# Writing out the steps of a biased attention with three routed trees, spacing the trees' groups four slots apart, and moving the routing of the last tree ahead of the end of the attention

## The chip, the cores and the metric

The kernel runs on one core of one Trainium2 chip. The time is the device time of one execution in microseconds (us). The kernel before was timed three times: 751.34, 752.47 and 753.41 us, median 752.47.

## What is computed

The input x is (4, 512, 128). It is normalised over its last axis (xn), and two branches are added to x.

```
xn  = (x - mean) / sqrt(var + 1e-5)
# branch 1: attention, 16 heads of 8, 512 tokens, 4 batches
q,k,v = split(xn @ w_qkv.T);  s = q.k * 8**-0.5 + bias[bucket(k_pos - q_pos)]
a     = softmax(s) @ v @ w_proj.T + b_proj
# branch 2: four hard-routed trees q, k, v, f of depth 8 (256 leaves, 16 hidden units each)
fff(x, act): node = 0; 8 times: node = 2*node + 1 + (x.nw[node] + nb[node] > 0)
             leaf = node - 255;  return act(x @ w1[leaf] + b1[leaf]) @ w2[leaf] + b2[leaf]
xm  = (xn - mean) / sqrt(std + 1e-5)
y   = xm + softmax(fff_q(xm) . fff_k(xm) / sqrt(128)) @ fff_v(xm)      # relu inside
b   = y + fff_f(y)                                                     # exact gelu inside
out = x + a + b
```

The last tree (f) works on y, so it can be routed only after the softmax over the outputs of the other three.

## The kernel before, in words

All five engines run one program each, ordered by semaphores and written out by hand. There is no planner: what stands next to what is set by small tables.

**The attention** (branch 1) is 16 steps: 4 batches times 4 groups of 4 heads (`n = 4 * b + g`). A step has 20 slots. In slots 0 to 15 TensorE computes one tile of scores of step n (`scores_k`, L1037 and L1039) for which ScalarE takes the exponent (`exps`, L824); in slots 4 to 19 it computes one tile of scores of step n + 1 (`scores_q`, L1026), of which VectorE takes the row maximum (`row_max`, L636); at slots 6, 10, 14 and 18 it multiplies by the values (`weigh`, L1049). Between two steps stand `max_rows` (L1066), `sub_max` on VectorE (L642, which every next step waits for), `split_k`, `split_q` and `normalise`; after every fourth step comes `output` (L1085, L1091). Score banks are used in pairs, so TensorE can be two tiles ahead of VectorE and of ScalarE and no more. The first 12 steps are in loops of three turns (`Fori`) on TensorE, VectorE and ScalarE, the last four steps stand written out.

**The trees** sort the 2048 tokens into 48 tiles of 128 by blocks of 8 leaves: VectorE routes (`route`, L546 to L607), TensorE counts (`ranks`, L968), GpSimd scatters the rows to DRAM with 16 indirect DMAs (`scatter`, L412). Four tiles are a group, so a tree has 12 groups. A group has four stages on TensorE: x (transposes, L1100), h (first product, L1106), m (mask, L1111), y (second product, L1116). ScalarE copies after x and takes the activation after h, VectorE masks after m and copies after y. SyncE loads the rows and the four weight blocks of a group two groups ahead (`turn`: `rows` L263, four register loads of block numbers L268, four weight DMAs L272) and stores the result (L283). GpSimd gathers a finished tree from DRAM with 16 indirect DMAs (`gather`, L417). Trees q, k and v ride in the attention's first 12 steps, three groups to a step, at the slots of `STAGES`.

**The attention of branch 2** (16 tiles, `attention`, L1158 s, L1164 p, L1177 o) rides in steps 12 to 14, a tile every two slots, after eight blocks of transposes (`qk_in`, L1129). Its `o` uses bank WB, its `p` bank 7.

**The last tree** is routed in step 15 (`y_transposed` L1137, `y_logits` L1147, `route_y` L679) and scattered after it. Its 12 groups have a schedule of their own (`F_PE`, `F_DVE`): six sets of buffers (`FG = 6`), two banks for each stage, the weight DMAs shared between SyncE and ScalarE. At the end GpSimd gathers, adding into `acc`, while SyncE stores each batch of `out` as soon as its four gathers have landed.

Of the kernel before, what the change touches and what calls it, by code (L numbers as in the profile page):

```python
# [20 lines left out]
F32 = mybir.dt.float32  # L21
F32R = mybir.dt.float32r
BF16 = mybir.dt.bfloat16
# [5 lines left out]
P = 128  # L29
# [18 lines left out]
GPS = GROUPS // NG  # L48
# [10 lines left out]
STAGES = [(0, "x0"), (2, "h0"), (4, "m0"), (5, "x1"), (6, "y0"), (8, "h1"), (10, "m1"), (11, "x2"), (12, "y1"),  # L59
          (14, "h2"), (16, "m2"), (19, "y2")]  # L60
# [9 lines left out]
          "yl": 1, "hr": 1, "hh": 1, "hm": 1, "mk": 1, "yy": 1, "st": 16,  # L70
          "f_xs": 2, "f_h": 2, "f_hr": 2, "f_hm": 2, "f_y": 2, "f_yl": 2, "f_st0": 16, "f_st1": 16}
FG = 6
F_PE = "x0 x1 h0 m0 x2 h1 m1 x3 y0 h2 m2 x4 y1 h3 m3 x5 y2 h4 m4 y3 h5 m5 y4 y5".split()
F_DVE = "x0 x1 x2 m0 x3 m1 y0 x4 m2 y1 x5 m3 y2 m4 y3 m5 y4 y5".split()
# [8 lines left out]
def attend(delays, tree, g, at):  # L83

    if tree is not None:
        return []
    return [(k, sum(ATT_TILES[:g]) + r) for r in reversed(range(ATT_TILES[g])) for k, d in delays.items()
            if ATT_FROM[g] + 2 * r + d == at]
# [5 lines left out]


def stages(tree, g, at):

    return [] if tree is None else [(what[0], GPS * g + int(what[1])) for slot_, what in STAGES if slot_ == at]

# [7 lines left out]
def build(nc, x, wq, wk, wv, wp, bp, table, onehot, cf, cb, nw, nb, wl, b2, out):  # L107
# [7 lines left out]
    with ctx:  # L115
        def sb(name, shape, dt=F32):
# [58 lines left out]
        end = strip[:].rearrange("p a b -> p (a b)").bitcast(F32)  # L175
        nw_f, nb_f = end[:, 0:NODES], end[:, NODES:2 * NODES]
        bits_f, work_f = end[:, 1024:3072], end[:, 3072:5120]
# [10 lines left out]

        f_wt = end[:, 0:FG * GT * WROW].rearrange("p (q t c) -> p q t c", q=FG, c=WROW)
        f_xl = yt[:].rearrange("p a b c -> p (a b c)")[:, 0:FG * GT * ROW].rearrange("p (q t c) -> p q t c", q=FG, c=ROW)  # L190
        f_xTs, f_hr, f_hm, f_yl = (tuple(pt[:, k // 2, k % 2 * 2 + i].rearrange("p (t c) -> p t c", c=P)
                                         for i in range(2)) for k in range(4))

        ps = ctx.enter_context(nc.psum_tensor("ps", [P, 8, NS], F32))
        OB, WB = 4, 6
# [1152 lines left out]
```

## Time and profile before

| | us |
|---|---|
| median of three runs | 752.47 |
| the profiled execution, its own time | 751.0 |
| its span, first to last instruction | 748.9 |
| TensorE busy | 576.3 (77%) |
| VectorE busy | 455.4 (61%) |
| ScalarE busy | 299.5 (40%) |
| GpSimd busy | 254.9 (34%) |
| mean granted TensorE clock | 0.90 |

Busy time of TensorE is modelled and counts overlapping work as full, so a row of instructions is best read by the distance of their starts. "PEld" is a weight load of TensorE, "DVE" VectorE, "ACT" ScalarE, "POOL" GpSimd, "SPq" the queue of SyncE. "L412" is line 412 of the kernel.

### The profile page before, as it was taken

To read this page: it belongs to the slowest core of one execution; us is meant where nothing else is said; L and a number is where in the kernel's file an instruction comes from. 1 tells how busy PE (TensorE), PEld (TensorE's weight loads), DVE (VectorE), ACT (ScalarE), POOL (GpSimd) and SP (SyncE) were. 2 spreads that over 40 slices of the span, in tenths; PEclk is the share of its full clock that TensorE was granted. 3 is DMA by queue.
4 is the path that set the end of the run, shared out by engine and by line. 5 is a ranking of instruction groups with operands and counts; after the bars stand their busy time and mean duration, and the time that the engine had idled before them with its cause. 6 is when DMAs were issued, how large, how long until landed. Compare 5 with 4: busy or idle time off the path is not lost.

```text
span 748.9 us, 12769 instructions
## 1 busy us (share of the span) xinstructions
PE 576.3 (77%) x3522; PEld 417.0 (56%) x3540; DVE 455.4 (61%) x1036; ACT 299.5 (40%) x703; POOL 254.9 (34%) x239
## 2 busy tenths in 40 slices
PE   1185465999999999999999999994999996174800
PEld 0173332666776667667667676663666674074800
DVE  3979887576676667776667767752656667033500
ACT  4510010655555446546455465471555523021300
POOL 4403667710000768700183000084000000787075
PEclk9786876999999999999999999997999999576955
DMA  7979341444344466744475443121000000779333
GB/s 219 271 164 277 125 118 46 110 128 124 104 113 114 122 170 141 147 113 112 105 146 128 117 110 94 51 36 22 1 0 1 1 15 4 221 173 303 88 46 68
DMA packets 108825, 83.30 MB, mean 111 GB/s; under 512 B 8688, under 2 KB 105840, under 8 KB 108768
## 3 DMA queue, kind: packets, MB, share of 16 engines
q1 hardware_dynamic: 89952, 66.91, 33.0%
q0 software_dynamic: 15104, 12.63, 9.1%
q10 hardware_dynamic: 3712, 3.16, 1.5%
q14 instruction: 41, 0.34, 0.2%
q8 instruction: 16, 0.26, 0.1%
HBM read 58.30 MB, written 24.36 MB: 110 GB/s over the span
## 4 chain that ended last, share of the span: by engine, by line
PE 44%; issue 21%; POOL 7%; DVE 4%; ACT 3%; DMA 2%; SPq 2%; DVEq 0%; POOLq 0%; ACTq 0%
PE ps L1049 7%; PE ps L1026 6%; PE ps L1037 6%; PE ps L1039 6%; PE ps L1106 5%; PE ps L1116 3%; PE ps L1009 3%; POOL acc L417 3%; DVE ps L636 2%; POOL yt L417 2%; PE ps L1100 2%; POOL xs L412 2%; DMA ys<-pt 1%; PE ps L1262 1%; ACT hr L835 1%
## 5 line engine op out<-in xcount | busy, mean ns | idle before, releaser
L636 DVE CUSTOM_DVE_ANT_0 ps<-ps,strip 128x512 f32<-128x512 f32 x256 | 176.9, 704 | 116.7 <-PE ps L1026 112.5
L824 ACT ACTIVATE pt<-ps 128x512 f32<-128x512 f32 x256 | 148.9, 603 | 96.1 <-PE ps L1039 94.1
L412 POOL DMA_INDIRECT xs<-xr,slot x64 | 63.3, 990 | 254.7 <-issue 137.6
L417 POOL DMA_INDIRECT yt<-ys,slot x48 | 74.2, 1547 | 155.3 <-DMA ys<-yl 141.3
L1037 PE MATMUL ps<-qs,km 128*128 128x512 f32 x256 | 121.5, 475 | 3.3 <-ACT pt L824 1.7
L1026 PE MATMUL ps<-km,qs 128*128 128x512 f32 x256 | 108.2, 436 | 11.9 <-DVE qs L619 5.4
L1039 PE MATMUL ps<-u_lo,rev_r 128*128 128x220 f32 (+1 forms) x256 | 74.3, 290 | 0.0
L1039 PE MATMUL ps<-u_hi,rev_r 128*128 128x220 f32 (+1 forms) x256 | 72.8, 284 | 0.0
L1049 PE MATMUL ps<-pt,v_aug 128*32 128x512 f32 x512 | 68.2, 605 | 0.7 <-ACT pt L824 0.7
L1026 PEld LDWEIGHTS ps<-km,qs 128*128 128x128 f32 x256 | 48.7, 194 | 35.0 <-DVE mx L636 27.5
L1037 PEld LDWEIGHTS ps<-qs,km 128*128 128x128 f32 x256 | 48.8, 191 | 17.4 <-ACT pt L824 9.7
L1039 PEld LDWEIGHTS ps<-u_lo,rev_r 128*128 128x128 f32 x256 | 48.2, 188 | 11.3
L835 ACT ACTIVATE hr<-ps,wt 128x128 f32<-128x128 f32 x144 | 41.2, 369 | 31.9 <-PE ps L1106 31.9
L417 POOL DMA_INDIRECT yt<-in_b,leaf x48 | 46.0, 958 | 19.6 <-issue 14.0
L1039 PEld LDWEIGHTS ps<-u_hi,rev_r 128*128 128x128 f32 x256 | 49.0, 191 | 4.1 <-issue 2.2
L1116 PEld LDWEIGHTS ps<-wt,hm 128*128 128x128 f32 x288 | 36.8, 191 | 11.1 <-issue 10.1
L1106 PEld LDWEIGHTS ps<-xTs,wt 128*128 128x128 f32 x288 | 35.9, 191 | 12.6 <-issue 12.0
L1106 PE MATMUL ps<-xTs,wt 128*128 128x128 f32 x288 | 39.4, 280 | 1.7 <-ACT xTs L830 1.7
L1116 PE MATMUL ps<-wt,hm 128*128 128x128 f32 x288 | 39.2, 279 | 0.0
L965 PE MATMUL ps<-v_all,yt 128*128 128x256 f32 x96 | 26.9, 440 | 13.8 <-DVE pt L594 8.7
L636 DVE DVE_READ_ACCUMULATOR2_ANT mx<- 128x1 f32 x256 | 36.3, 142 | 0.0
L671 DVE COPY yl<-ps 128x512 f32<-128x512 f32 x36 | 24.9, 692 | 16.9 <-PE ps L1116 15.2
(218 smaller groups left out, 903.5 us busy)
## 6 DMA issues: line engine op xcount, KB each, us to landing
wt<-in_wl SPq DMA_DIRECT2D x144, 128.5 KB
xl<-xs SPq DMA_DIRECT2D x36, 258.0 KB
ys<-yl SPq DMA_DIRECT2D x36, 256.0 KB, 2.8
xs<-mx SPq DMA_DIRECT2D x2, 3096.0 KB, 22.8
strip<-bias_bf SPq DMA_DIRECT2D x1, 3584.0 KB, 36.4
yt<-xs SPq DMA_DIRECT2D x12, 258.0 KB, 5.3
strip<-in_wl SPq DMA_DIRECT2D x24, 128.5 KB, 3.4
strip<-in_wl ACTq DMA_DIRECT2D x24, 128.5 KB, 3.6
```

The lines of the kernel that those rows point to most:

```text
L412: pool.indirect_dma_start(out=xs[t % 2][:, :], out_offset=bass.IndirectOffsetOnAxis(ap=slot[:, t, k:k + 1], axis=0), in_=xr[:, k, :], in_o ...
L417: pool.indirect_dma_start(out=dst, out_offset=None, in_=src[:, :], in_offset=bass.IndirectOffsetOnAxis(ap=idx, axis=0), compute_op=op).the ...
L636: V.tensor_tensor_reduce(out=bank(u % banks), in0=bank(u % banks), in1=strip[:, HG * g + j, b0:b0 + NS], scale=1.0, scalar=LOWEST, op0=ALU ...
L824: A.activation(pt[:, kt % 2, j, :], bank(2 + u % 2), ACT.Exp).then_inc(S["ex"], 1)
L835: last = A.activation(hr[:, i, :], ps[:, BB[k], i * P:(i + 1) * P], ACT.Relu, bias=wt[:, par, i, 2 * P:WROW])
L965: last = T.matmul(ps[:, k, i * NODES:(i + 1) * NODES], src[:, (2 * k + i) * P:(2 * k + i + 1) * P], w, start=True, stop=True)
L1026: T.matmul(bank(u % banks), qs[:, par, qt * P:(qt + 1) * P], backward(km[:, par, j, :]), start=True, stop=True).then_inc(S["p1"], 1)
L1037: T.matmul(bank(2 + u % 2), km[:, par, j, kt * P:(kt + 1) * P], qs[:, par, :], start=True, stop=False)
L1039: last = T.matmul(ps[:, 2 + u % 2, lo:hi], rev_r[:], half[:, HG * g + j, u0:u0 + hi - lo], start=False, stop=stop)
L1049: last = T.matmul(ps[HR * j:HR * j + HR, OB, :], v_aug[:, par, kt, j, :], pt[:, kt % 2, j, :], start=kt == 0, stop=kt == KT - 1)
L1106: last = T.matmul(quarter(BB[k], i), wt[:, par, i, 0:P], xTs[:, i, :], start=True, stop=True)
L1116: last = T.matmul(quarter(BB[k], i), hm[:, i, :], wt[:, par, i, P:2 * P], start=True, stop=True)
```

## The change

- The loops over the first 12 steps (and those of SyncE over a tree's groups) are gone: all 16 steps are written out, and semaphore values and offsets are constants.
- A group of a tree starts every four slots (`EVERY = 4`), five to a step, with x at its slot 0, h at 2, m at 3 and y at 5. The 36 groups of trees q, k and v thus fill slots 0 to 145 of the 320, seven and a quarter steps instead of twelve.
- `qk_in` stands at slots 150 to 164. The 16 tiles of the second attention start every two and a half slots from slot 167; `p` and `o` both use bank 7 now, and `p` waits until the tile before it has been taken out of that bank.
- The last tree is routed from slot 209 on: VectorE takes one piece of `route_y` after each slot's other work (it is a generator now), TensorE has its transposes at slots 209 and 210, the logits at 212 to 218, the ranks at 223. The scatter and the gather of b2 (now into `xr`) follow on GpSimd.
- The last tree's groups are the 37th to 48th of the one common schedule. They start behind the last step (`F_FROM = 322`), with the two sets of buffers, one bank pair and one SyncE `turn` that the other trees have.
- The final gather adds into `xr`; GpSimd adds `xr` to `acc` per batch after it, and only then is that batch stored.
- `normalise` stands at slot 2 instead of ahead of slot 0 on VectorE. All transposes of the attention use bank WB.

```diff
-STAGES = [(0, "x0"), (2, "h0"), (4, "m0"), (5, "x1"), (6, "y0"), (8, "h1"), (10, "m1"), (11, "x2"), (12, "y1"),
-          (14, "h2"), (16, "m2"), (19, "y2")]
-FG = 6
-F_PE = "x0 x1 h0 m0 x2 h1 m1 x3 y0 h2 m2 x4 y1 h3 m3 x5 y2 h4 m4 y3 h5 m5 y4 y5".split()
-QK_AT = (1, 2, 4, 5, 7, 8, 10, 11)
-ATT_TILES, ATT_FROM = (2, 7, 7, 0), (12, 3, 3, 0)
-ATT_PE, ATT_DVE, ATT_ACT = {"s": 0, "p": 2, "o": 3}, {"s": 0, "o": 4}, {"s": 1, "p": 2}
+STEPS = NB * NG
+STAGE_AT = {"x": 0, "h": 2, "m": 3, "y": 5}
+EVERY = 4
+QK_FROM, ATT_FROM, ROUTE_FROM, F_FROM = 150, 167, 209, 322
+ATT_PE, ATT_DVE, ATT_ACT = {"s": 0, "p": 2, "o": 4}, {"s": 0, "o": 4}, {"s": 1, "p": 2}
+def stages(slot_):
+    found = []
+    for what, d in STAGE_AT.items():
+        for first, start, count in ((0, 0, NTREE * GROUPS), (NTREE * GROUPS, F_FROM, GROUPS)):
+            k, rest = divmod(slot_ - start - d, EVERY)
+            if rest == 0 and 0 <= k < count:
+                found.append((what, first + k))
+    return found
+def attend(delays, slot_):
+    return [(k, i) for i in range(NT) for k, d in reversed(delays.items()) if ATT_FROM + 5 * i // 2 + d == slot_]
...
+            def turn(n, last):
+                if n + 2 < last:
...
                     sp.wait_ge(S["mk"], n + 1 + CREDIT["mk"])
-                    rows(nxt[0], nxt[1], par)
+                    rows(n + 2)
                     block_of = blocks(n + 2)
                     sp.wait_ge(S["yy"], n + 1 + CREDIT["yy"])
-                    weights(block_of, par)
+                    weights(block_of, n % 2)
+                t, m = divmod(n, GROUPS)
                 sp.wait_ge(S["yl"], n + 1 + CREDIT["yl"])
...
+            for n in range(NTREE * GROUPS, (NTREE + 1) * GROUPS):
+                turn(n, (NTREE + 1) * GROUPS)
             for b in range(NB):
-                sp.wait_ge(S[f"g_o{b}"], 16 * KT)
+                sp.wait_ge(S["y_add"], b + 1)
+                sp.wait_ge(S["acc"], b + 1 + CREDIT["acc"])
                 sp.dma_start(out[b].rearrange("(t p) c -> p t c", p=P), acc[:, b * KT:(b + 1) * KT, :]).then_inc(S["d_out"], 16)
...
             for k in range(NT):
-                fetch(acc[:, k, :], ys[0], slot[:, TF, k:k + 1], ALU.add, S[f"g_o{k // KT}"])
+                fetch(xr[:, k, 0:P], ys[0], slot[:, TF, k:k + 1], ALU.add, S[f"g_o{k // KT}"])
+            for b in range(NB):
+                pool.wait_ge(S[f"g_o{b}"], 16 * KT)
+                pool.wait_ge(S["acc"], b + 1 + CREDIT["acc"])
+                part = slice(b * KT, (b + 1) * KT)
+                G.tensor_tensor(acc[:, part], acc[:, part], xr[:, part, 0:P], ALU.add).then_inc(S["y_add"], 1)
...
+            def step(n):          # VectorE
...
+                for at in range(SLOTS):
+                    if at == 2 and g > 0:
+                        normalise(n - 1, b, g - 1)
+                    if at >= LAG and nxt:
+                        row_max(n + 1, (g + 1) % NG, at - LAG)
+                    for k, i in stages(slot_of(n, at)):
+                        stage(k, i)
+                    for k, i in attend(ATT_DVE, slot_of(n, at)):
+                        attention(k, i)
+                    if slot_of(n, at) >= ROUTE_FROM:
+                        next(route_f, None)
...
                 elif k == "p":
                     pe.wait_ge(S["s_ex"], i + 1)
-                    pe.wait_ge(S["qs2"], n + 1)
+                    if i > 0:
+                        pe.wait_ge(S["y_sb"], i)
...
+            def route_y(after):   # TensorE
+                for k in {0: (0, 1), 1: (2, 3)}.get(after, ()):
+                    y_transposed(k)
+                for k in {3: (0, 1), 4: (2,), 5: (3,), 6: (4,), 7: (5,), 8: (6,), 9: (7,)}.get(after, ()):
+                    y_logits(k)
+                if after == 14:
+                    ranks(TF, work_f, FB)
...
-            with pe.Fori(0, NTREE) as b:
-                for g in range(NG):
-                    step(b, g, (b, g + 1) if g + 1 < NG else (b + 1, 0), b)
...
+            for n in range(STEPS):
+                step(n)
+            for at in range(STEPS * SLOTS, F_FROM + GROUPS * EVERY + EVERY):
+                for k, i in stages(at):
+                    stage(k, i, i % 2)
```

## Rows read from the trace of the kernel before

**Rows 1.** Busy time per window: start:end, length, PE, PEld, DVE, ACT, POOL, clock, DMA share, GB/s
```profile
454.21:482.94 28.73, 28.07 (x181) 20.10 (x181) 19.98 (x48) 15.64 (x35) 0.00 (x0) 1.00 0.26 74
...
482.94:525.60 42.66, 31.37 (x181) 21.70 (x181) 19.09 (x49) 18.09 (x35) 24.68 (x16) 0.88 0.23 32
525.60:563.59 37.99, 35.74 (x207) 23.89 (x207) 23.49 (x63) 19.53 (x41) 0.00 (x0) 1.00 0.00 1
...
601.57:627.60 26.03, 24.11 (x132) 17.97 (x134) 19.58 (x35) 9.22 (x17) 0.00 (x0) 0.93 0.04 11
627.60:656.20 28.60, 5.88 (x47) 4.48 (x46) 5.88 (x21) 2.46 (x3) 15.48 (x16) 0.60 0.51 149
656.20:712.80 56.60, 39.17 (x288) 37.40 (x288) 24.02 (x36) 13.72 (x48) 28.88 (x18) 0.80 0.74 187
712.80:748.90 36.10, 0.00 (x0) 0.00 (x0) 0.00 (x0) 0.00 (x0) 24.66 (x16) 0.50 0.34 58
```
**Rows 2.** Timeline, step 12: start, length, engine, line, operation, idle before it, releaser
```profile
486.07 1.56 POOL L417 DMA_INDIRECT yt<-ys,slot  x1 [86.30 <-DMA ys<-yl]
...
517.07 2.05 PE L1177 MATMUL ps<-yt,b_pT 128*128 128x128 f32 x8 [9.54 <-issue]
```
**Rows 3.** Timeline, the first ScalarE instruction behind a loop's jump
```profile
253.58 0.60 ACT L830 ACTIVATE xTs<-ps 128x512 f32<-128x512 f32 x1 [2.54 <-PE ps L1100]
```
**Rows 4.** Timeline: slot starts on TensorE, plain and with second-attention work; a tile's end on VectorE
```profile
321.09 0.48 PE L1037 MATMUL ps<-qs,km 128*128 128x512 f32 x1
...
321.92 0.40 PE L1037 MATMUL ps<-qs,km 128*128 128x512 f32 x1
...
538.79 0.47 PE L1037 MATMUL ps<-qs,km 128*128 128x512 f32 x1
...
539.43 0.35 DVE L693 SCALAR_TENSOR_TENSOR xr<-ps,st,xr 128x128 f32<-128x128 f32 x1
...
540.77 0.48 PE L1037 MATMUL ps<-qs,km 128*128 128x512 f32 x1
...
542.82 0.47 PE L1037 MATMUL ps<-qs,km 128*128 128x512 f32 x1
```
**Rows 5.** Timeline: slot starts on TensorE in step 15, the eighth and the sixteenth
```profile
617.74 0.50 PE L1037 MATMUL ps<-qs,km 128*128 128x512 f32 x1
...
625.05 0.50 PE L1037 MATMUL ps<-qs,km 128*128 128x512 f32 x1
```
**Rows 6.** Timeline of VectorE in step 11, last instruction ahead of the row maxima
```profile
459.42 0.29 DVE L652 TENSOR_TENSOR att<-ps,rc 128x128 f32<-128x128 f32 x1
```
**Rows 7.** Costliest groups of the page: busy us, mean ns, idle before
```profile
L636 DVE CUSTOM_DVE_ANT_0 ps<-ps,strip 128x512 f32<-128x512 f32 x256 | 176.9, 704 | 116.7 <-PE ps L1026 112.5
```
**Rows 8.** Timeline of VectorE: the last routing after its comparisons
```profile
617.06 0.18 DVE L562 TENSOR_SCALAR strip<-strip 128x16 bf16<-128x16 bf16 x1
...
629.99 0.19 DVE L586 TENSOR_SCALAR whole<-ps 128x32 int32<-128x32 f32 x1 [1.59 <-PE ps L980]
...
634.16 0.15 DVE L606 TENSOR_SCALAR ewc<-sm 128x1 int32<-128x1 f32 x1
```
**Rows 9.** Timeline of SyncE's queue: two ungated loads of a group's rows
```profile
88.91 0.37 SPq L263 DMA_DIRECT2D xl<-xs  x1
...
94.53 0.53 SPq L263 DMA_DIRECT2D xl<-xs  x1
```
**Rows 10.** Instructions of line L218: durations in ns, min/median/max
```profile
L218 SPq TENSOR_LOAD <-ew x24: 263/278/1085, 636.1 to 688.8; - x24
```
**Rows 11.** Timeline: the last group of the last tree, first product and last copy
```profile
704.75 1.06 PE L1262 MATMUL ps<-pt,strip 128*128 128x128 f32 x8
...
709.02 0.69 DVE L760 COPY pt<-ps 128x512 f32<-128x512 f32 x1 [0.65 <-PE ps L1273]
```
**Rows 12.** Timeline of GpSimd: its add, and the last gather
```profile
656.23 4.16 POOL L450 TENSOR_TENSOR acc<-acc,xr 128x2048 f32<-128x2048 f32 x1 [1.58 <-DMA xs<-xr,slot]
...
740.49 1.54 POOL L417 DMA_INDIRECT acc<-ys,slot  x1 [0.30 <-issue]
```

More of the change, by code:

```diff
@@ L299, in f_rows @@
-            def f_rows(m, q):
-                sp.dma_start(f_xl[:, q], xs[TF % 2][bass.ds(m * GT * P, GT * P), :].rearrange("(t p) c -> p t c", p=P)
-                             ).then_inc(FX[q], 16)
             sp.wait_ge(S["d_ew0"], 16)
             sp.wait_ge(S["d_sc"], 16 * NT)
-            for par in range(2):
-                rows(0, par, par)
-                weights(blocks(par), par)
-            for t in range(NTREE):
-                tree(t, t + 1 < NTREE)
-            sp.wait_ge(S["max"], U * NB * NG + CREDIT["max"])
@@ L313, in _ @@
-            sp.dma_start(nw_f, nw[:, TF, :]).then_inc(S["d_n"], 16)
+            for n in range(2):
+                rows(n)
+                weights(blocks(n), n)
+            for n in range(NTREE * GROUPS):
+                turn(n, NTREE * GROUPS)
+            sp.wait_ge(S["s_ex"], KT)
+            sp.dma_start(nw_f, nw[:, TF, :]).then_inc(S["d_nf"], 16)
             sp.dma_start(nb_f, bass.AP(tensor=nb.tensor, offset=TF * NODES, ap=[[0, P], [1, NODES]])
-                         ).then_inc(S["d_n"], 16)
+                         ).then_inc(S["d_nf"], 16)
@@ L967, in logits, with ranks @@
                     last.then_inc(S["lg"], 1)
-            def ranks(t, work):
+            def ranks(t, work, rank):
                 wb = work.bitcast(BF16)
@@ L1090, in output, with stage @@
                 for k in range(KT):
-                    last = T.matmul(quarter(TB(NG - 1), k), attT[:, k * P:(k + 1) * P], wp_s[:], start=True, stop=True)
+                    last = T.matmul(quarter(WB, k), attT[:, k * P:(k + 1) * P], wp_s[:], start=True, stop=True)
                 last.then_inc(S["pr"], 1)
-            def stage(k, n, half, par):
+            def stage(k, n, par):
+                half = n // 2
                 if k == "x":
@@ new lines, in step @@
+                        project(n + 1, (n + 1) // NG, (n + 1) % NG, 1)
+                for at in range(SLOTS):
+                    if (EARLY if g == 0 else 0) <= at < U:
+                        scores_k(n, g, at, par)
+                    if at == 0 and nxt and g > 0:
+                        project(n + 1, (n + 1) // NG, (n + 1) % NG, 0)
+                    if at == 2 and g > 0:
+                        tokens_first(n - 1)
+                    if at >= LAG and nxt:
+                        scores_q(n + 1, at - LAG, 1 - par)
+                    if at >= WEIGH_AT and (at - WEIGH_AT) % HG == 0:
+                        weigh(n, (at - WEIGH_AT) // HG, par)
+                    for k, i in stages(slot_of(n, at)):
+                        stage(k, i, i % 2)
+                    for t in qk_at(slot_of(n, at)):
+                        qk_in(t)
+                    for k, i in attend(ATT_PE, slot_of(n, at)):
+                        attention(k, i)
+                    route_y(slot_of(n, at) - ROUTE_FROM)
```

420 lines of the change are left out of this document (139 added, 281 removed), and 2 rows, old and new, of the table S.

## The prediction

> **What bounds the kernel now.** I read the page's slices first (TensorE near full from the seventh slice to the thirtieth, then a tail in which no engine is), then the windows between the steps' `sub_max`, then the timeline inside single steps. The windows [rows 1] are the frame of the sum, and the reader is to see four things in them. A step that carries three groups takes 28.7 us and TensorE is busy in 28.1 of it: there the attention is bound by TensorE. Step 12 takes 42.7 us with only 31.4 busy: it holds a stall. Step 15 takes 26.0 us with VectorE busy for 19.6 of it. Behind 627.6 come 121.3 us of tail in three stages: 28.6 (end of the routing, scatter), 56.6 (the last tree's groups) and 36.1 (gather and store, TensorE idle).
>
> The work left in the attention must be known per slot. A plain slot lasts 0.83 us; two slots with a tile's s, p and o last 1.98 + 2.05 [rows 4]. So a tile of the second attention costs 4.03 - 1.66 = 2.37 us, and a bare step is 37.99 - 7 x 2.37 = 21.4 us [rows 1]. A group costs (28.73 - 21.4) / 3 = 2.4 us.
>
> **The change part by part.** The sum is made on the profiled execution (751.0 us, span 748.9, 2.1 around it).
>
> 1. *Groups closer together.* The 36 groups cost TensorE the same 2.4 us wherever they stand, so 0. Five to a step make it 21.4 + 12.2 = 33.6 us, 6.7 per group. VectorE then has 20.0 + 2 x 1.4 = 23 us of work in it, so TensorE stays the bound. Range -3 (the slack at step ends is filled) to +4 (a store or a weight block comes late).
>
> 2. *The stall in step 12.* The first o waits 9.5 us for the third tree's gather, which runs from 486.07 to 517.07, 31 us [rows 2]. Now that tree's last y is at slot 145 and the first o at slot 171. Between them lie 26 slots (26/20 x 21.4 = 28 us), eight transposes of 0.4, an `output` of about 3 and two tile beginnings: some 36 us. Against it stand 4.5 us for copy and store and the 31: 35.5. It just fits: -9. Ends: 0 and -9.5.
>
> 3. *Loops gone.* Behind a loop's jump ScalarE's first copy came after 2.5 us of idleness [rows 3], where about 1.2 of it were the transposes before it. There are two jumps back. -1; ends 0 and -3.
>
> 4. *p and o in one bank.* In a pair of tiles the second p follows the first o in the same slot and has to wait until VectorE has taken o out: the reciprocal, the 0.35 us of L693 [rows 4] and the hops, together 0.85 us, during which TensorE has nothing else in order. Eight pairs make 6.8; some of it falls where TensorE would have waited anyway. +6; ends +2 and +9.
>
> 5. *Routing in step 15 goes.* From the step's start (601.57, plus 0.74 to the first slot) to the eighth slot it took 15.4 us; the eight slots from there to the last took 7.3, with two `weigh` [rows 5]. Seven slots with one `weigh` at that pace are 6.2. -9.2.
>
> 6. *Routing in steps 10 and 11 comes.* In step 10 it is the same transposes and logits on TensorE, in slots in which TensorE is the bound as well: +9. In step 11 the bound changes to VectorE. Its work from `sub_max` until `normalise` is done takes 459.71 - 454.21 = 5.5 us [rows 6]; then 16 row maxima at 0.75 each (0.704 and the reading of the accumulator) [rows 7], 12.0; then the routing behind the comparisons, 617.06 to 634.31 less the 1.6 it waited for the ranks, 15.7 [rows 8]; the transposes before the next `sub_max`, 0.7. That is 33.9, and with two waits for TensorE (first score tile, ranks) 35.4, against 21.4 for the bare step: +14. TensorE cannot run ahead of it, since the score banks allow two tiles. At slot 223 TensorE waits some 5 us for the one-hot rows: in step 12, after 9.5 us of idleness, the clock of the step was 0.88 and its matmuls took twice as long (2.05 for eight) [rows 1, 2]; +1 for that. Together +24. Ends: +18 (step 10 half hidden) and +30 (each piece behind TensorE's slot, clock low).
>
> 7. *The tail until the gather.* Before, 627.6 to 712.8, 85.2 us. After: from the end of step 15 six short hops (copy, transposes, `normalise`, transposes, copy, projection, 0.6 to 1.2 each) 4.5; the first group until its mask 2.9. From then on a group takes what SyncE's `turn` takes. Two ungated loads of rows stand 5.6 us apart [rows 9], with one row DMA, four register loads and four weight DMAs between them, and these were first issues, some 0.5 slow; a store of 0.45 and three waits come to it: 5.8. TensorE's own chain (h, activation, x of the next group in the same bank, y, h again) is near 4.2 at 2.4 GHz, an estimate from the last group, where h took 1.06 and h to the last copy 5.0 [rows 11]; so SyncE is the bound. Nine turns are 52.2; the last weights have landed 8.1 after the last turn began (3.3 until the first weight DMA, 1.5 until the fourth, 3.3 to landing, as the page has it for the other indirect and weight DMAs); h to the last copy 5.0 (704.75 to 709.71) [rows 11]; store and start of the gather 3.1. Sum 4.5 + 2.9 + 52.2 + 8.1 + 5.0 + 3.1 = 75.8, and 0.5 for a low clock. -8.9. The scatter and routing that leave (28.6) are thus mostly paid back by groups at 5.8 instead of 56.6/12 = 4.7, and by a fill and drain without six sets of buffers. Ends: turn 5.4, -13; turn 7, +3.
>
> 8. *The closing adds.* The 128x2048 add took 4.16 [rows 12], so a quarter is 1.1. GpSimd starts them when its last gather is issued (740.49 + 1.54), does the first three while the last lands and ends the fourth 4.5 later, at 746.5 on the old scale. Before, the last batch could go 3.3 after the last gather's start, at 743.8. +2.7; ends +1 and +4.
>
> Sum: 0 - 9 - 1 + 6 - 9.2 + 24 - 8.9 + 2.7 = +4.6. The profiled execution would take 755.6; put on the median of 752.47 that is 757.
>
> The trace shows the register load of a block number at 278 ns in the median, up to 1085 [rows 10]. The Trainium skill, DMA: Bandwidth & Descriptors, "Latency and other measured facts", gives a tensor_load a floor of about 600 ns; the median of the trace is below it, its slowest above. By that page's figure a turn would be 4 x 0.32 = 1.3 us longer and the tail 12 us; this speaks against the change and stands beside rival B.
>
> **The rivals.**
>
> *A, faster: VectorE's routing hides.* The place is step 11. If TensorE's waits there overlap with the row maxima better than I count, step 10 costs 5 instead of 9, step 11 12 instead of 14 and the waits of point 4 only 2: 8 to 11 us less, and the whole is 747 to 749. For it: VectorE is idle for 8.7 us in a loaded step [rows 1]. Against it: a bare step is 21.4 long with 17.5 of VectorE's own work (5.5 + 12.0). It decides from the point where points 4 and 6 together stay under 25.
>
> *B, slower still: the turn is longer.* After the row DMA the next register load took up to 1.09 us [rows 10]; with one such load a turn and one more late, a turn is 6.8 and nine make +9: 766. For it: the long ones were all in the tail, under traffic. Against it: after's tail moves 1.03 MB a group in 5.8 us, 178 GB/s, under the 187 of the same stage before [rows 1].
>
> *C, the stall stays.* If the gather starts 5 us later than I count or the slots run faster, o waits again: +5, 762. Then the change does not do one of the things it says.
>
> *D, nothing to be seen.* The parts cancel: 750 to 754.
>
> **How the numbers follow.** What a measurement of this kernel can tell from no change is about 0.3%, 2.3 us. Forecast (755 to 761) 0.40, all slower; A 0.27, faster; B 0.10 and C 0.07, slower; D 0.16, within. So faster 0.27, same 0.16, slower 0.57. The range that leaves out no more than 2 in 10 reaches from A to B: 745 to 768; the forecast's own range is 752 to 762.
>
> **What would show it.** Point 2: no idle time over 1 us before the first o. Point 4: about 0.85 us of idle TensorE before every second p. Point 6: the step from slot 220 near 35 us, with VectorE over 90% busy, the step before it some 9 longer than its tiles explain. Point 5: step 15 near 17 us. Point 7: the SyncE row loads of the last tree 5.8 us apart, TensorE released by the weights' landing. Point 8: four adds of 1.1 in a row behind the last gather. If the attention ends before 632 us of the span, or the tail behind it is shorter than 110, the sum is wrong on that side.

## The result and the profile after

| | median of 4 runs | lowest to highest | profiled execution | its span |
|---|---|---|---|---|
| before | 751.9 us | 749.45 to 753.41 | 751.0 us | 748.9 us |
| after | 765.99 us | 762.49 to 766.79 | 765.5 us | 763.8 us |

The ratio of the times is 1.0182, with a 95% interval of 1.0139 to 1.0224: slower by 1.8%, and 14.9 us in the spans of the two profiled executions, where the sum had said 4.6.

The windows of the kernel after, cut at the starts of `sub_max` on VectorE, at the end of the attention (645.76) and at the start of the last gather (723.07); columns as in [rows 1]:

```profile
166.07:199.78 33.71, 33.04 (x230) 25.27 (x229) 22.25 (x51) 18.96 (x45) 0.00 (x0) 1.00 0.56 148
...
435.60:478.18 42.58, 38.00 (x222) 25.72 (x221) 25.23 (x66) 21.15 (x44) 0.00 (x0) 1.00 0.00 1
478.18:517.50 39.32, 35.54 (x206) 25.25 (x205) 26.40 (x66) 14.93 (x29) 0.00 (x0) 1.00 0.00 1
517.50:558.19 40.69, 28.51 (x142) 16.43 (x141) 29.07 (x77) 11.24 (x20) 6.36 (x7) 0.86 0.07 19
...
606.77:629.19 22.42, 20.40 (x109) 12.19 (x107) 15.96 (x41) 11.20 (x20) 0.00 (x0) 1.00 0.00 1
629.19:645.76 16.57, 14.34 (x84) 8.60 (x84) 1.24 (x3) 9.08 (x17) 0.00 (x0) 1.00 0.00 1
645.76:723.07 77.31, 50.83 (x304) 41.06 (x304) 18.54 (x27) 23.36 (x63) 0.00 (x1) 0.88 0.53 144
723.07:763.80 40.73, 0.00 (x0) 0.00 (x0) 0.00 (x0) 0.00 (x0) 29.28 (x20) 0.50 0.30 52
```

They answer to [rows 1]. Steps count from 0. A step with five groups takes 33.71 us (forecast 33.6). Step 9, eight tiles and no group, takes 42.58, and TensorE is idle in 4.6 of it. Step 11, which holds the routing, takes 40.69 (forecast 35.4); VectorE is busy for 29.07 of it, so it isn't the full bound it was taken for. A step with nothing added takes 22.42 (taken: 21.4). Step 15 takes 16.57. The attention ends 18.2 us later than before (645.76 against 627.58), the stretch until the gather is 7.9 shorter (77.3 against 85.2), and the closing 4.6 longer (40.7 against 36.1): 18.2 - 7.9 + 4.6 = 14.9.

The first o of the second attention, on TensorE's timeline of the kernel after, answers to [rows 2]. It starts at 417.17 with no idle time in front of it; on GpSimd's timeline the gather it needs ran from 383.93 and issued its last part at 411.89. The stall is gone:

```profile
416.94 0.40 PE L963 MATMUL ps<-km,qs 128*128 128x512 f32 x1
417.17 1.05 PE L1107 MATMUL ps<-yt,b_pT 128*128 128x128 f32 x8
```

SyncE's queue behind the attention, after, answers to [rows 9]. The loads of rows (L255) stand 5.19, 5.68 and 6.19 us apart, in the mean of the nine turns 5.77 ((707.27 - 655.36) / 9), between them the index loads, four weight DMAs and a store:

```profile
660.55 0.51 SPq L255 DMA_DIRECT2D xl<-xs  x1
663.78 1.93 SPq L264 DMA_DIRECT2D wt<-in_wl  x4
665.75 0.43 SPq L280 DMA_DIRECT2D ys<-yl  x1
666.23 0.51 SPq L255 DMA_DIRECT2D xl<-xs  x1
669.76 2.14 SPq L264 DMA_DIRECT2D wt<-in_wl  x4
671.95 0.43 SPq L280 DMA_DIRECT2D ys<-yl  x1
672.42 0.51 SPq L255 DMA_DIRECT2D xl<-xs  x1
```

The end of GpSimd's timeline, after, answers to [rows 12]: four adds, all of them behind the sixteenth gather.

```profile
750.79 1.54 POOL L386 DMA_INDIRECT xr<-ys,slot  x1 [0.31 <-issue]
751.78 5.15 POOL L428 TENSOR_TENSOR acc<-acc,xr 128x512 f32<-128x512 f32 x4
```

### The profile page after: what moved, and what is told of

The parts are those of the page before. It is cut to its first block, busy times and chain, and to the rows that moved or that the text cites. A ratio compares the mean times of both kernels' runs of the same rounds, so it can differ in the third digit from the quotient of the medians.

```text
span 763.8 us, 11493 instructions
## 1 busy us (share of the span) xinstructions
PE 588.9 (77%) x3540; PEld 417.9 (55%) x3540; DVE 443.9 (58%) x1024; ACT 310.4 (41%) x715; POOL 255.6 (33%) x242
## 4 chain that ended last, share of the span: by engine, by line
PE 56%; DVE 9%; SPq 6%; issue 5%; POOL 4%; ACT 3%; DMA 1%; POOLq 0%; DVEq 0%; ACTq 0%
PE ps L986 8%; PE ps L963 7%; PE ps L974 7%; PE ps L976 7%; PE ps L1040 5%; PE ps L1050 5%; POOL xr L386 3%; PE ps L946 3%; SPq L260 3%; DVE ps L617 3%; SPq L264 2%; PE ps L1093 2%; PE ps L1045 2%; PE ps L1034 2%; PE ps L1001 1%
## 5 line engine op out<-in xcount | busy, mean ns | idle before, releaser
L974 PE MATMUL ps<-qs,km 128*128 128x512 f32 x256 | 126.0, 492 | 3.1 <-ACT pt L786 2.1
L963 PE MATMUL ps<-km,qs 128*128 128x512 f32 x256 | 111.4, 444 | 17.0 <-DVE mx L617 9.7
L797 ACT ACTIVATE hr<-ps,wt 128x128 f32<-128x128 f32 x192 | 54.9, 369 | 93.5 <-PE ps L1040 93.5
L386 POOL DMA_INDIRECT xr<-ys,slot x16 | 24.7, 1543 | 126.4 <-DMA ys<-yl 121.8
L1040 PEld LDWEIGHTS ps<-xTs,wt 128*128 128x128 f32 x384 | 47.6, 195 | 34.7 <-issue 24.6
L1040 PE MATMUL ps<-xTs,wt 128*128 128x128 f32 x384 | 55.8, 289 | 9.0 <-DMA wt<-in_wl 8.2
L1050 PE MATMUL ps<-wt,hm 128*128 128x128 f32 x384 | 55.1, 288 | 2.8 <-DVE hm L647 1.3
L652 DVE COPY yl<-ps 128x512 f32<-128x512 f32 x48 | 33.1, 691 | 39.0 <-DMA ys<-yl 36.3
L1050 PEld LDWEIGHTS ps<-wt,hm 128*128 128x128 f32 x384 | 50.6, 199 | 9.1 <-DVE hm L647 8.1
L647 DVE SCALAR_TENSOR_TENSOR hm<-ps,cst,hr 128x512 f32<-128x512 f32 x48 | 35.9, 749 | 28.0 <-ACT hr L797 19.7
```

The costliest lines, as they stand in the source:

```text
L386: pool.indirect_dma_start(out=dst, out_offset=None, in_=src[:, :], in_offset=bass.IndirectOffsetOnAxis(ap=idx, axis=0), compute_op=op).the ...
L647: V.scalar_tensor_tensor(flat(hm[:]), bank(BB[k]), col(C_LEAF), flat(hr[:]), ALU.is_equal, ALU.mult).then_inc(S["hm"], 1)
L797: last = A.activation(hr[:, i, :], ps[:, BB[k], i * P:(i + 1) * P], ACT.Relu if n < NTREE * GROUPS else ACT.Gelu, bias=wt[:, par, i, 2 * P ...
L963: T.matmul(bank(u % banks), qs[:, par, qt * P:(qt + 1) * P], backward(km[:, par, j, :]), start=True, stop=True).then_inc(S["p1"], 1)
L974: T.matmul(bank(2 + u % 2), km[:, par, j, kt * P:(kt + 1) * P], qs[:, par, :], start=True, stop=False)
L1040: last = T.matmul(quarter(BB[k], i), wt[:, par, i, 0:P], xTs[:, i, :], start=True, stop=True)
```

## The experiments

Steps are compared by their lengths (from one `sub_max` to the next) in the profiles, where an undisturbed step repeats within 0.05 us; medians and ratios are against the kernel before, run on the same chip. "Attention" is the sum of the sixteen steps: 497.6 us before, 515.9 after.

**1. The kernel before with its outer loop written out** (nothing else changed):

```
-            with dve.Fori(0, NTREE) as b:
+            for b in range(NTREE):        # likewise on ScalarE and TensorE
```

> The kernel before with only its first twelve steps written out on TensorE, VectorE and ScalarE (the tables and the last tree stay as they were; SyncE keeps its loops). Theory: two jumps back cost 1 us each at most, so -1 to -2 us against before (751). Rival: jumps cost more (each engine idles 2.5 us at the seam for them), -4 us or more. Second rival: written-out code is slower, above 752.

748.28 us against 749.95, ratio 0.996 (0.9935 to 0.9985). The step behind the first jump back falls from 32.16 to 31.18, the one behind the second from 31.46 to 31.19: 1.25 together, near the 1 of point 3 and within the theory's two; the rival of 4 and more falls. The attention as a whole is 2.0 us shorter in the profiled execution, but the rest of that is not shown to be the loops'. The last step falls from 26.01 to 24.42, and in it the execution of before was granted a clock of 0.76 up to 604.00 and of 0.63 from there to 607.00 of its span, where this one was granted 1.00 throughout. TensorE had waited the same 1.00 and 0.78 us just ahead, in both. The transposes of y (L1137), before and in this run:

```profile
602.87 2.55 PE L1137 MATMUL ps<-cst,xr 128*128 128x128 f32 x11
...
604.08 1.47 PE L1137 MATMUL ps<-cst,xr 128*128 128x128 f32 x12
```

The first step rises from 30.87 to 31.78, with a clock of 0.97 before and 0.94 here. Two executions that differ in their clock there say nothing of the loops.

**2. The kernel after, o one slot earlier:**

```
-ATT_PE, ATT_DVE, ATT_ACT = {"s": 0, "p": 2, "o": 4}, {"s": 0, "o": 4}, {"s": 1, "p": 2}
+ATT_PE, ATT_DVE, ATT_ACT = {"s": 0, "p": 2, "o": 3}, {"s": 0, "o": 3}, {"s": 1, "p": 2}
```

> The changed kernel with o of the second attention one slot earlier on TensorE and VectorE, so that the next p stands a slot behind it. Theory: the 0.85 us that every second p waited is gone, 8 x 0.85 = 6 to 7 us off 766: about 760. Rival: the wait was filled by what VectorE and ScalarE had left over, and it stays at 766 (-1 or less).

763.71 us, ratio 1.0202 (1.014 to 1.0265); the attention is only 0.6 us shorter than after's, step 9 42.12. The theory's 6 to 7 us did not come. Read by itself this says that the shared bank costs nothing, and the expectation of experiment 9 has that as its rival. But in step 9 of this kernel p still waited 2.1 us for VectorE, and its loads now waited 3.5 for ScalarE: the wait had in part changed its name. Experiment 9 takes the cause away.

**3. The kernel after, the last routing behind the sixteen steps:**

```
-                    if slot_of(n, at) >= ROUTE_FROM:
-                        next(route_f, None)
...
+            for _ in route_f:      # behind the loop over the steps; TensorE's part likewise
+                pass
```

> The changed kernel with the whole routing of the last tree behind the last step. Theory (routing under the attention costs 28 us, VectorE-bound in step 11): steps 10 and 11 fall from 39.3 and 40.7 to about 30 and 24 us (step 11 a bare one plus its few extras), the attention ends at 618 instead of 646 of the span, and behind it come 25 of routing and 22 of scatter: 785 in all. Rival (most of the surplus is in packing and tiles, routing costs 15): the attention ends at 631, 798 in all.

792.08 us (one run). Steps 10, 11 and 12 take 31.31, 22.44 and 24.72 in place of 39.32, 40.69 and 26.09: the routing under the attention costs 8.0 + 18.25 + 1.4 = 27.6 us, as the theory said (28; the rival's 15 falls). Step 11 of this kernel is the bare step:

```profile
508.61:531.05 22.44, 20.45 (x110) 12.46 (x109) 15.97 (x41) 11.21 (x20) 0.00 (x0) 1.00 0.00 1
```

Behind the attention the routing, the scatter and what follows take 54 us more than after's tail (172.0 against 118.0), so to hide it was right even at 27.6. The whole came out 7 us above the 785 of the theory, which had taken 47 for routing and scatter.

**4. The kernel after, a piece of routing every third slot:**

```
-                    if slot_of(n, at) >= ROUTE_FROM:
+                    if slot_of(n, at) >= ROUTE_FROM and (slot_of(n, at) - ROUTE_FROM) % 3 == 0:
```

> The changed kernel with a piece of the last routing after every third slot (slots 209 to 284) instead of after every slot, on VectorE and TensorE alike. Theory: a bare step leaves VectorE some 5 us idle, so 3.75 steps hide some 15 of the 25 us of pieces: routing costs 13 instead of 28 us, 751 in all, and no step from 10 to 14 is over 33 us. Rival: every piece holds up the next row maximum and with it TensorE wherever it stands, so that the cost per piece stays: 764 to 767.

758.22 us, ratio 1.0106 (1.0067 to 1.0144). The attention is 9.9 us shorter than after's, so the same pieces cost some 17.7 spread over five steps: between the theory's 13 and the rival's unchanged 27.6, and step 10 takes 35.25 where the theory had no step over 33. Its steps 10 and 11:

```profile
480.09:515.34 35.25, 30.53 (x182) 20.86 (x181) 22.39 (x58) 14.94 (x29) 0.00 (x0) 1.00 0.00 1
515.34:541.61 26.27, 25.12 (x134) 16.94 (x133) 19.82 (x48) 11.33 (x20) 0.00 (x0) 1.00 0.00 1
```

A bare step has 15.97 us of VectorE's own work (experiment 3). With a piece in every slot the routing's comes on top, and TensorE, held to two score banks, waits for VectorE again and again. With a piece in every third, TensorE is busy for 25.12 of 26.27. A part of the 9.9 is the clock: step 11 of after was granted 0.86 (point 6 below), all these steps 1.00. How much of it is the one and how much the other was not separated.

**5. The kernel after, four groups a step:**

```
-EVERY = 4
-QK_FROM, ATT_FROM, ROUTE_FROM, F_FROM = 150, 167, 209, 322
+EVERY = 5
+QK_FROM, ATT_FROM, ROUTE_FROM, F_FROM = 186, 203, 245, 322
```

> A group every fifth slot, so four in an undisturbed step; query rows, attention and routing start 36, 36 and 36 slots later. Theory (a fifth group costs a step more than the third did, 2.25 us each with five against 2.09 with three, because the cover in the slots is used up): undisturbed steps of four come out at 31.0 us (22.44 + 4 x 2.14), the 36 groups cost 77 us in place of 81.1 and the attention ends 3 to 5 us earlier. Rival (the price of a group is the same 2.25 however many there are): steps of 31.4 and no gain. The routing falls into steps that hold attention tiles but no groups; its whole cost should stay near the 27.5 us found by moving it behind the steps. Span 759 to 763 by the theory, 763 to 765 by the rival.

769.67 us (one run). An undisturbed step takes 31.86: 22.44 + 4 x 2.36. Neither line is met: four groups cost more each than five (2.25) and than before's three (2.09). The columns of TensorE tell why:

```profile
197.55:229.41 31.86, 30.42 (x206) 22.62 (x205) 21.12 (x49) 17.66 (x40) 1.09 (x2) 1.00 0.50 135
```

TensorE is busy for (30.42 - 20.45) / 4 = 2.49 us more per group than in the bare step, with before's three it is 2.54 and with after's five 2.52: a group costs it the same. What differs is the idle time that the step keeps: 1.99 bare, 1.44 with four groups at every fifth slot, 0.67 with five at every fourth, 0.66 with before's three. So the price of a group depends on where its x, h, m and y fall in a step, not only on how many there are. Which slots leave the idle time was not tried. The attention is 2.9 us longer than after's, not 3 to 5 shorter, and the span 767.9, above both lines; where the rest of that goes was not followed up.

**6. The kernel after, the closing of before** (GpSimd's four closing adds go; one early add and the gathers of b2 into `acc` take their place):

```
+            G.tensor_tensor(acc[:], acc[:], xr[:, :, 0:P], ALU.add).then_inc(S["y_add"], 1)
...
-                fetch(xr[:, k, 0:P], ys[0], slot[:, TF, k:k + 1], ALU.add, S[f"g_o{k // KT}"])
+                fetch(acc[:, k, :], ys[0], slot[:, TF, k:k + 1], ALU.add, S[f"g_o{k // KT}"])
```

> The closing of the kernel before is put back: the x rows are added to acc early, the rows of b2 and the last gather add straight into acc, and each quarter of the output is stored when its own four gathers have landed. Theory (the four late additions on GpSimd, 5.15 us together, and the bunched stores behind them are what the closing stretch lost): from the start of the last gather to the end 36.1 us in place of 40.7, so 4.6 us less in all, 761. Rival (GpSimd issues the gathers late anyway and the additions lie beside their landings): under 1.5 us less, 765.

763.5 us, ratio 1.0189 (1.0156 to 1.0222). From the gather's start to the end it takes 36.1 us, 4.6 less than after, as the theory said to the tenth, though the whole stayed above its 761:

```profile
725.78:761.90 36.12, 0.00 (x0) 0.00 (x0) 0.00 (x0) 0.00 (x0) 24.67 (x16) 0.50 0.34 58
```

The whole gained only 1.9 in the span, since the attention began 1.4 later in this execution and the stretch ahead of the gather took 78.8 in place of 77.3. The edit moved more than the adds: GpSimd now issues its sixteen gathers of b2 behind the attention, from 657.39 to 686.68, and not under it. The five turns of SyncE's queue beside them, from 656.64 on, take 30.6 us together where after's first five take 28.6; the four behind them take 23.4 and 23.3. So the old closing gives 4.6 back at the end and costs up to 2 in the groups; no run moved those gathers by themselves.

**7. The kernel after with one index load a group behind the attention** (it leaves out that each tile has its own block: all four of a group get the first tile's weights):

```
+                if n >= NTREE * GROUPS + 2:
+                    return [sp.value_load(ew[0:1, n * GT:n * GT + 1], min_val=0, max_val=4 * BLK - 1)] * GT
```

> In the last tree's groups SyncE reads one block index a group in place of four and uses it for all four weight loads; what it leaves out: the weights of three tiles of four, so those rows get another block's product. Theory (SyncE's own instructions set the turn of a group behind the attention, 5.8 us between two row loads): the turn falls to 4.9 us or less with three index loads of 0.3 us less, and the eight turns left give 7 us or more. Rival (the weights' landing and the chain h, m, y, copy, store bound the turn): it stays within 0.2 of 5.8 and the span within 1.5 us of 763.8.

756.33 us (one run), the span 9.2 under after's, as the theory said (7 or more). SyncE's queue:

```profile
667.01 0.50 SPq L255 DMA_DIRECT2D xl<-xs  x1
668.50 1.78 SPq L266 DMA_DIRECT2D wt<-in_wl  x4
670.33 0.42 SPq L282 DMA_DIRECT2D ys<-yl  x1
670.91 0.39 SPq L255 DMA_DIRECT2D xl<-xs  x1
```

The turns take 4.69 in the mean ((699.40 - 657.20) / 9, between 3.9 and 5.5), 1.08 less for three index loads, 0.36 each. SyncE's own instructions do set the turn, as point 7 said. The Trainium skill, DMA: Bandwidth & Descriptors, "Latency and other measured facts", gives such a load a floor of about 600 ns, by which three would have been 1.8; this run shows less.

**8. The kernel after, the last tree's groups 60 slots earlier:**

```
-QK_FROM, ATT_FROM, ROUTE_FROM, F_FROM = 150, 167, 209, 322
+QK_FROM, ATT_FROM, ROUTE_FROM, F_FROM = 150, 167, 209, 262
```

> The last tree's groups start 60 slots earlier, one every fourth slot under steps 13 to 15 and what follows, in place of behind the attention. Theory (behind the attention they take 5.8 us each with TensorE idle most of that; under a step they cost what a group cost earlier, 2.1 to 2.3 us, plus the ScalarE table loads that Exp and Gelu side by side need, 1.28 us each, two a group at most): 14 to 15 groups add 30 to 60 us to steps 13 to 15 and take some 70 from the tail; 726 to 750 in all, below the kernel before. Rival (ScalarE with its table loads and the exponentials sets the pace): the steps grow by 5 us a group and the total stays at 760 or above.

726.73 us, ratio 0.9711 (0.9677 to 0.9744): below the kernel before. (There are 12 such groups; the expectation said 14 to 15. Nor is TensorE "idle most of" the time behind the attention of after: it is busy for 50.83 of 77.31.) Steps 13 to 15 take 32.70, 39.29 and 29.32 in place of 22.49, 22.42 and 16.57: 39.8 us for 12 groups, 3.3 each in place of 5.8, and the gather starts at 683.80, before the attention ends (685.33). What they cost more than the 2.25 of earlier groups is in part ScalarE's: in step 14 it is busy for 32.59 of 39.29, and the waits view has TensorE behind its exponentials for 2.3 us and TensorE's weight loads for 3.3. Another part is the clock, 0.96 in that step; the same five groups took 37.23 at a clock of 1.00 in experiment 12. ScalarE's timeline in step 14:

```profile
643.42 0.60 ACT L786 ACTIVATE pt<-ps 128x512 f32<-128x512 f32 x1 [0.79 <-PE ps L976]
644.03 1.28 ACT L797 ACT_TABLE_LOAD   x1
645.33 1.14 ACT L797 ACTIVATE hr<-ps,wt 128x128 f32<-128x128 f32 x4
646.49 1.28 ACT L786 ACT_TABLE_LOAD   x1
647.78 1.09 ACT L786 ACTIVATE pt<-ps 128x512 f32<-128x512 f32 x2
```

The last tree's activation is Gelu, the attention's Exp, and each change of one for the other is a table load of 1.28 us, two a group, eleven in this step; with the other trees' Relu the trace of after has none in step 1. The Trainium skill, ScalarE: Activation LUTs, "What ACT_TABLE_LOAD costs", gives 1283 ns for the load, which this trace shows to the digit, and 1380 ns of drain beside it, which it does not show: from the end of Exp (644.02) to the start of Gelu (645.33) it is 1.31.

**9. The kernel after, o in the bank it had before:**

```
-                        last = T.matmul(quarter(BB["m"], 0), b_pT[:, k_ * P:(k_ + 1) * P], yt[:, 2, b_ * KT + k_, :],
+                        last = T.matmul(quarter(WB, 0), b_pT[:, k_ * P:(k_ + 1) * P], yt[:, 2, b_ * KT + k_, :],
```

with the waits that sharing `WB` with the row maxima and the token transposes needs, and without p's wait for the o ahead of it.

> The o of a tile of the second attention goes back into the bank in which it was before (the one the row maxima and token transposes use), p keeps its own; the next p no longer waits for VectorE to take o out. Theory (one bank for p and o costs 0.85 us at every second tile, point 4 of the prediction): a step of eight tiles falls from 42.6 to 39 to 41, and the attention ends 4 to 6 us earlier, span 758 to 760. Rival (after a first test in which o one slot earlier gave 0.5 us, what a tile costs more than before, 2.52 against 2.22 us, comes from the pitch of 2.5 slots, which puts tiles into the step's first and last slots): 42.6 stays within 0.5 and the attention ends within 1 us of 645.8; waits at the step's ends for the shared bank can even make it 1 to 2 us longer.

756.03 us, ratio 1.0073 (1.0049 to 1.0097). The attention is 9.5 us shorter than after's: steps 8, 9 and 10 take 35.09, 37.79 and 37.30 in place of 37.73, 42.58 and 39.32. The theory has the place and the cause, and is too small (4 to 6; 39 to 41 for step 9). The same step 9:

```profile
433.12:470.91 37.79, 37.39 (x222) 25.77 (x221) 25.27 (x67) 21.15 (x44) 0.00 (x0) 1.00 0.00 1
```

TensorE does the same 222 matmuls and is idle for 0.4 us in place of 4.6. The rival, that the pitch of tiles (the distance between their starts) costs it, falls. The timeline of the kernel after, TensorE and VectorE at two tiles of step 9, shows how (L1107 is o, L673 and L674 take it out, L1100 is the next p):

```profile
438.19 1.07 PE L1107 MATMUL ps<-yt,b_pT 128*128 128x128 f32 x8
440.16 0.15 DVE L673 RECIPROCAL st<-st 128x1 f32<-128x1 f32 x1
440.35 0.35 DVE L674 SCALAR_TENSOR_TENSOR xr<-ps,st,xr 128x128 f32<-128x128 f32 x1
440.85 0.63 PE L1100 MATMUL ps<-cst,xl 128*128 128x128 f32 x4 [1.59 <-DVE xr L674]
...
449.23 1.16 PE L1107 MATMUL ps<-yt,b_pT 128*128 128x128 f32 x8
450.43 0.16 DVE L673 RECIPROCAL st<-st 128x1 f32<-128x1 f32 x1 [1.18 <-PE ps L1107]
450.62 0.35 DVE L674 SCALAR_TENSOR_TENSOR xr<-ps,st,xr 128x128 f32<-128x128 f32 x1
451.12 0.63 PE L1100 MATMUL ps<-cst,xl 128*128 128x128 f32 x4 [0.73 <-DVE xr L674]
```

Where VectorE is free, p waits 0.73 us; where VectorE comes late to the reciprocal, without idle time before it, 1.59. The waits view of that step adds these up over its eight tiles: five of the p's waited, 4.6 us together. Over all sixteen tiles ten waited, 9.2 us, which is the 9.5 that the bank of its own gave back.

**10. The last groups from slot 254, and 11. the closing adds on VectorE as well:**

```
-QK_FROM, ATT_FROM, ROUTE_FROM, F_FROM = 150, 167, 209, 322
+QK_FROM, ATT_FROM, ROUTE_FROM, F_FROM = 150, 167, 209, 254
```
```
-                pool.wait_ge(S[f"g_o{b}"], 16 * KT)
...
-                G.tensor_tensor(acc[:, part], acc[:, part], xr[:, part, 0:P], ALU.add).then_inc(S["y_add"], 1)
...
+                dve.wait_ge(S[f"g_o{b}"], 16 * KT)      # behind VectorE's last group
...
+                V.tensor_tensor(acc[:, part], acc[:, part], xr[:, part, 0:P], ALU.add).then_inc(S["y_add"], 1)
```

> As the kernel whose last groups started at slot 262, but at 254. There the scatter's last issue was 570.0 and the first x would now come near 576, so nothing should wait. Theory (the end is set by the gather's start, which follows the last group's slot, not by the attention's end): 8 slots of step 15 at 1.47 us are 12 us; the last gather starts near 672 in place of 683.8, the attention still ends at 685 within 2 us, the total is 714 to 717 in place of 726.7. Rival (rows or weights come late for the first groups behind the scatter, or the attention grows by what the gather's traffic slows): 720 to 725.

> As the kernel with the last groups from slot 254, and the four closing additions are VectorE's, each as soon as its quarter's gathers have landed, in place of GpSimd's behind all sixteen. Theory (GpSimd starts the additions only when its last gather is issued, and the four take 5.15 us and bunch the stores): the first three additions and stores go beside the gathers, the last one ends 3 to 4 us earlier than GpSimd's; total 710 to 714. Rival (the last gather's landing and the last store of 6.5 us set the end, the additions lay beside them): less than 1.5 us under the kernel with the additions on GpSimd.

718.91 us, ratio 0.9573 (0.9513 to 0.9634), and 712.24 us, 0.9517 (0.9475 to 0.9558). In the first the gather starts at 675.61, 8.2 us earlier than in experiment 8 where 12 were forecast (1.3 of the 8.2 is the attention's earlier start in that execution), and the attention still ends at 684.78: the gather's start sets the end, but the eight slots gave less, between the two lines. In the second, the gather starts 2.9 earlier still, which is not the adds' doing, and from its start to the end it takes 36.4 us in place of 40.7: the adds gave 4.3, a little over the theory's 3 to 4, and the rival falls. VectorE's adds there lie beside the gathers:

```profile
687.65 0.69 DVE L722 TENSOR_TENSOR acc<-acc,xr 128x512 f32<-128x512 f32 x1
688.92 0.69 DVE L722 TENSOR_TENSOR acc<-acc,xr 128x512 f32<-128x512 f32 x1 [0.58 <-DMA xr<-ys,slot]
696.46 0.69 DVE L722 TENSOR_TENSOR acc<-acc,xr 128x512 f32<-128x512 f32 x1 [6.84 <-DMA xr<-ys,slot]
703.98 0.69 DVE L722 TENSOR_TENSOR acc<-acc,xr 128x512 f32<-128x512 f32 x1 [6.83 <-DMA xr<-ys,slot]
```

**12. All that helped in one kernel** (experiments 9 and 11 together):

> Everything that has helped, in one kernel: o in its own bank, the last groups from slot 254, the closing additions on VectorE. Theory (the three places are apart: the bank acts in steps 8 to 10, the groups in 12 to 15, the additions at the end): 712.2 less 9.5 = 703, at most 2 us to either side. Rival (what the bank gains is lost again where the scatter's indirect DMAs, 1.27 us each whatever the attention does, become late for the first of the last groups): 707 to 711, with a wait for rows in step 12.

704.36 us (703.08 to 705.96), ratio 0.9388 (0.9354 to 0.9422): 6% under the kernel before, within 2 us of the theory's 703. Step 14, five groups with Gelu, and the tail:

```profile
614.91:652.14 37.23, 32.84 (x226) 25.00 (x226) 22.98 (x53) 32.64 (x56) 0.00 (x0) 1.00 0.50 135
674.19:701.40 27.21, 2.44 (x16) 1.81 (x16) 3.92 (x7) 1.19 (x2) 17.27 (x11) 0.61 0.38 67
```

## Why the prediction was right in sign and too small in size

| point | forecast | measured | from |
|---|---|---|---|
| 1 groups closer together | 0 | +5.7 | steps of after, experiment 3 |
| 2 stall | -9 | gone, about -9.5 | first o |
| 3 loops | -1 | -1.3 | experiment 1, the steps behind the jumps |
| 4 p and o in one bank | +6 | +9.5 | experiment 9 |
| 5 step 15 | -9.2 | -9.4 | 26.01 to 16.57 (1.6 of it the clock) |
| 6 routing in steps 10 to 12 | +24 | +27.6 | experiment 3 |
| 7 tail until the gather | -8.9 | -7.9 | 85.2 to 77.3 |
| 8 closing adds | +2.7 | +4.6 | experiment 6 |
| not in the sum: pitch of tiles | | -4.8 | below |

The measured column adds up to +14.5, against 14.9 in the spans. What is left, 0.4, I don't place. It is less certain than it looks: the rows come from one profiled execution each, and the 1.6 us of low clock in step 15 (experiment 1) belong to before's execution, in the forecast as in the measured row. The low clock behind the stall (2.05 us for an o [rows 2] that takes 1.05 after) went with the stall and stands in no row.

**The step that failed is point 1**, "the 36 groups cost TensorE the same 2.4 us wherever they stand, so 0". It rests on a bare step of 21.4 us, reached by subtracting seven tiles as two slots show them [rows 4]. The bare step is 22.44; it was measured in after's form alone, as the kernel before has no step without groups or tiles, and for before it is taken over. With that, a group before cost (28.73 - 22.44) / 3 = 2.09, and one after (33.71 - 22.44) / 5 = 2.25: 36 x 0.16 = 5.7. The 5.7 doesn't hang on what before's bare step would be: twelve steps of three groups are 344.8 us, twelve bare steps of after and 36 groups at 2.25 are 350.4.

For TensorE's busy time the sentence of the prediction holds (2.54 and 2.52 us a group, experiment 5). What it left out is idle time. Counted with the same bare step, each step that holds groups fills 1.3 of the 2.0 us that the bare one idles; before, twelve steps did so, after only seven and a quarter, and 4.8 x 1.33 = 6.4, less 36 x 0.02, is the 5.7 again. The prediction had that slack as its -3, with the sign the other way. This is read off the busy columns; no run changed the closeness alone.

The forecast of the loaded step (33.6 against 33.71) came out right by luck, as the group too dear made up for the step too short; only the difference between the kernels, which the sum needs, was lost. The stated upper end of +4 was too low too. A tile's price in the kernel before is, with the same bare step, (37.99 - 22.44) / 7 = 2.22, not 2.37.

**Point 4** had the mechanism and its place, and was mis-sized: 9.5 in place of 6, just over its upper end. Counted were eight p's at 0.85 us, less what would fall into other waits; ten waited, 0.50 to 1.59 us each and 0.92 in the mean, and next to nothing of it fell into other waits. Beside it was a gain nobody had counted: with its own bank a tile of the new pitch costs (37.79 - 22.44) / 8 = 1.92, so the pitch saved 16 x 0.3 = 4.8; there TensorE idles for 0.4 us of the step, in before's for 2.25. That price comes from one step and was not tested by itself. The Trainium skill, Perfetto Trace Analysis, "Matmuls", says that independent groups of matmuls should rotate through different banks of PSUM so that reading one out overlaps the next group's products; experiment 9 prices the exception at 9.5 us for 16 tiles.

**Point 6**: step 10 cost 8.0 where 9 was forecast, step 11 18.25 where 14 was. "The bound changes to VectorE" is half true. Its busy time in step 11 is 29.07, under the 33.9 worked out, which had counted the 5.5 us from `sub_max` to the end of `normalise` as they elapsed, 1.2 us of waiting included. But it waits 11.6 us and not the 1.5 counted: the timeline of VectorE has 3.64 for the ranks, 1.83 and 1.21 at the end, 1.02 for k, and 0.2 to 0.4 before nearly every row maximum that follows a piece of routing. In this step two engines that hand each other work slot by slot are slower than the busier one alone. VectorE first, then TensorE:

```profile
530.62 0.70 DVE L617 CUSTOM_DVE_ANT_0 ps<-ps,strip 128x512 f32<-128x512 f32 x1 [3.64 <-PE ps L963]
...
536.25 0.70 DVE L617 CUSTOM_DVE_ANT_0 ps<-ps,strip 128x512 f32<-128x512 f32 x1 [0.22 <-PE ps L963]
537.77 0.70 DVE L617 CUSTOM_DVE_ANT_0 ps<-ps,strip 128x512 f32<-128x512 f32 x1 [0.21 <-PE ps L963]
...
556.23 0.70 DVE L617 CUSTOM_DVE_ANT_0 ps<-ps,strip 128x512 f32<-128x512 f32 x1 [1.83 <-PE ps L963]
```
```profile
525.72 0.39 PE L912 MATMUL ps<-yt,cbt 128*128 128x512 bf16 x1 [3.98 <-DVEq L541]
...
550.86 1.44 PE L963 MATMUL ps<-km,qs 128*128 128x512 f32 x2 [2.65 <-DVE mx L617]
...
553.38 1.94 PE L986 MATMUL ps<-pt,v_aug 128*32 128x512 f32 x8
```

TensorE's clock fell twice in this step, and the forecast had 1 us for one fall. After the 3.98 us for the one-hot rows it was 0.64 until 529.00; the ranks then took 3.2 us from their first to the next matmul, where experiment 4, with a wait of 0.34 in front and a clock of 1.00, has 2.3. Then a long piece of routing, 547.51 to 549.75 on VectorE (L577 to L586), left TensorE idle for 2.65 us, and it was granted 0.50, the level of 1.2 GHz, from 550.86 to the step's end at 558.19 and 0.54 up to 561.00. A `weigh` took 1.94 us there and not 1.06, and VectorE's waits of 1.83 and 1.21 are for that TensorE. TensorE is busy for 8.8 us in those ten; half of that, 4.4, is an estimate of the most that the second fall cost, and it would cover the 3.6 by which point 6 was too small. No run separates it from the handing over.

**Points 2, 3, 5 and 7** came out nearly as worked out; the turn of 5.8 us was 5.77, and experiment 7 shows its cause. **Point 8**: the four adds take 5.15 us from 751.78, some 1.3 each and not 1.1, and the four stores start close together behind them.

**The rivals.** A (747 to 749) needed points 4 and 6 to stay under 25; they are 37, and VectorE's routing does not hide. B named 766, which is the time measured, by a turn of 6.8, which did not come: the number was met by another mechanism and proves nothing. C fell with the stall, D with the result. The forecast's own range ended at 762, so the measured 766 lies outside it; it lies inside the wide one.

## What to carry to other kernels

Get the price of an added item from two windows that differ in nothing but its number, not from neighbouring slots: subtracting items at their slot price made the bare step look 1 us too short here. Then look at the idle time of both windows beside the busy time. Items fill the idle time of a step once, so packing them into fewer steps can cost more although each takes the engine just as long. When a resource (here a bank) is given up to make room, price the wait by the slowest reader with its queue, and test it by giving the resource back: moving the waiting instruction can just rename the wait. When long pieces are laid between two engines that work hand in hand, look at the clock behind each long wait as well. And when work is moved behind a covered stage, ask first whether its last part can begin under it; that was worth 39 us here (experiment 8), while the closeness of the first trees' groups cost 5.7 and can pay only through what it makes room for.

## What the runs showed of the hardware

- ScalarE changed between Gelu and Exp at 1.28 us each way with under 0.05 us around the load. Five groups with two changes each made a step 39.3 us long at a clock of 0.96 (experiment 8) and 37.2 at 1.00 (experiment 12), in place of 33.7 for five groups with Relu.
- SyncE's turn fell by 0.36 us for each index load left out. Four DMAs issued back to back took 1.78 to 2.14 us.
- Writing the loop out gave 0.98 and 0.27 us directly behind the two jumps back.
- With sixteen gathers on GpSimd's queue beside them, five turns of SyncE's queue took 30.6 us in place of 28.6 (experiment 6).
- In step 11 the granted clock was 0.64 just after TensorE had stood 3.98 us and 0.50 after it had stood 2.65 us; in step 12 of before it was 0.50 from 517.00 to 520.00, after 9.54 us of idleness [rows 2]. In step 15 of before it was 0.76 and then 0.63 after waits of 1.00 and 0.78 us, and 1.00 after the same two waits in experiment 1: what TensorE did directly before does not tell by itself whether the clock falls.
